# A decoder layer on one core: cross-attention's last eight pairs reordered in freed banks, and TensorE's expert slots written out

## What is computed

```
x = x + self_attention(layernorm(x))            # 16 heads, quantised weights and activations
x = x + cross_attention(layernorm(x), context)
x = x + experts(layernorm(x))                   # 8 experts, top 2, FF 688

def cross_attention(h, ctx):                    # 16 heads of width 128
    q = rmsnorm(h @ Wq) * gq                    # per head
    k = rmsnorm(ctx @ Wk) * gk;  v = ctx @ Wv
    p = softmax(q @ k.T / sqrt(128))            # 64 queries x 64 keys in each of the 32 sequences
    return (p @ v) @ Wo

def experts(x):
    top_v, top_i = top_k(x @ router_w.T, 2);  probs = softmax(top_v)
    y[e] = (silu(x @ gate[e].T) * (x @ up[e].T)) @ down[e].T
    return sum over the two chosen e of probs * y[e]
```

## Time and profile before

| | |
|---|---|
| Runs | 1113.59 us median of 3 (1110.93 to 1114.21) |
| The profiled execution | 1113.47 us; its span, first to last instruction: 1111.7 us |
| TensorE, VectorE, ScalarE, GpSimd busy in the span | 71%, 61%, 51%, 31% |
| Cross-attention's steps without projections | about 672 to 752 us of the span |
| Routing | 752 to 816 us |
| Expert slots | 816 to 1096 us |

### The profile page before, as it was taken

How to read it: one execution, slowest core, us unless ns; L and a number is a source line. 1 busy time by engine, 2 the same in 40 slices (tenths; PEclk the granted TensorE clock), 3 DMA queues, 4 the chain that set the end, 5 groups by cost and what they waited for, 6 DMA issues and landing times. The chain is left out here.

```text
span 1111.7 us, 27116 instructions
## 1 busy us (share of the span) xinstructions
PE 783.8 (71%) x10382; PEld 563.0 (51%) x10383; DVE 674.2 (61%) x1178; ACT 569.7 (51%) x863; POOL 342.0 (31%) x375
## 2 busy tenths in 40 slices
PE   0016677862336779998998997666269999999993
PEld 0015666752222235565665565556246666666662
DVE  4995788869773567778787775546833333333330
ACT  0145899983733555665666754433024444444441
POOL 0300555441420012323232323330034444444442
PEclk9997777676666999999999998995579999999997
DMA  4002666758000101101101001008265222222223
GB/s 138 0 0 77 225 243 234 253 213 317 0 0 1 36 19 27 40 3 40 41 3 40 28 15 41 2 2 313 76 255 196 36 37 37 38 38 38 38 33 95
DMA packets 40062, 90.86 MB, mean 82 GB/s; under 512 B 5264, under 2 KB 25488, under 8 KB 38128
## 3 DMA queue, kind: packets, MB, share of 16 engines
q1 hardware_dynamic: 29168, 76.22, 19.4%
q0 software_dynamic: 7488, 10.23, 5.8%
q10 hardware_dynamic: 3328, 3.28, 0.8%
HBM read 62.71 MB, written 29.10 MB: 83 GB/s over the span
## 5 line engine op out<-in xcount | busy, mean ns | idle before, releaser
L1464 DVE SCALAR_TENSOR_TENSOR hid<-psu,hid 128x688 f32<-128x688 f32 x39 | 34.1, 874 | 168.0 <-ACT hid L1328 164.2
L872 POOL TENSOR_TENSOR x_pf<-x_sc,x_rden 128x512 f32<-128x512 f32 x32 | 33.3, 1042 | 252.8 <-DVE x_rden L989 252.8
L1026 PE MATMUL xbank_q<-arena 128*128 128x512 f16 x384 | 96.5, 389 | 17.0 <-DVE q_hl L956 11.9
L1106 PE MATMUL xbank_a<-arena,x_o 128*128 128x256 f16 x768 | 95.8, 275 | 17.5 <-DVE x_o L966 17.5
L1328 ACT ACTIVATE hid<-psg 128x688 f32<-128x688 f32 x39 | 29.0, 743 | 134.8 <-PE psu L1531 134.8
L1106 PEld LDWEIGHTS xbank_a<-arena,x_o 128*128 128x128 f16 x768 | 72.7, 98 | 32.7 <-DVE x_o L966 25.0
L1531 PE MATMUL psg<-wgu,f_xT 128*128 x468 | 76.6, 314 | 16.9 <-issue 11.0
L1545 PE MATMUL fbank<-arena,hidT 128*128 (+1 forms) x702 | 87.2, 273 | 1.3 <-ACT f_y L1346 0.8
L886 ACT ACTIVATE sqq<-xbank_q 128x512 f32<-128x512 f32 x64 | 38.1, 595 | 91.8 <-PE xbank_q L1026 91.8
L1531 PE MATMUL psu<-wgu,f_xT 128*128 x468 | 75.2, 310 | 0.0
L1545 PEld LDWEIGHTS fbank<-arena,hidT 128*128 128x128 f16 (+1 forms) x702 | 63.4, 97 | 16.7 <-issue 10.2
(11 more groups left out here) (276 smaller groups left out, 1948.0 us busy)
## 6 DMA issues: line engine op xcount, KB each, us to landing
arena<-in_wgu SPq DMA_DIRECT2D x16, 688.0 KB, 5.7
gu_pair<-arena SPq DMA_DIRECT2D x16, 688.0 KB, 3.1
wgu<-gu_pair SPq DMA_DIRECT2D x8, 1376.0 KB
ao<-key_norms SPq DMA_DIRECT2D x64, 128.0 KB, 3.2
d_pair<-arena SPq DMA_DIRECT2D x16, 384.0 KB, 3.8
arena<-d_pair SPq DMA_DIRECT2D x8, 768.0 KB
arena<-in_wd SPq DMA_DIRECT2D x8, 384.0 KB, 5.5
x_sb<-in_x SPq DMA_DIRECT2D x2, 1024.0 KB, 9.4
```

What stands on the lines that cost most here:

```text
L1026: last = nc.tensor.matmul(bank_q[:, :], wq[:, a, k, f:f + D2], hT[:, b * NCH + k, at:at + GN], start=(j == 0), stop=(j == len(terms) - 1))
L1106: last = nc.tensor.matmul(acc[t // 2][:, (t % 2) * C:(t % 2 + 1) * C], o_hl[h % 2][:, a, at:at + P], wvo[:, b, e, :], start=(e == 0 and j ...
```

## The change

Cross-attention, from TAIL = 24 on. The banks of query and key projections become one tensor `qk` of two banks. The scores of pairs 0 to 24 stay in `xbank_s`, those of 25 to 31 go to `xbank_n`, which the norms have left. The weighted sums of odd heads from 47 on go to `qk`, the others to `xbank_o`; `attend(h)` then waits for the low half of head h - 2. Every engine's order in steps 24 to 31 changes, with the scores now two pairs ahead; step 23 takes pair 25's scores and softmax at its end, and the projection of head 46 moves from step 23 to step 24. In the experts TensorE's 41 slot steps are written out in Python instead of the loop, and the register with the expert's number is kept for the down product two slots later. The diff, cut to what differs in order, banks and waits (ScalarE's and GpSimd's bodies only moved into functions):

```diff
+TAIL = NPAIR - NU
...
-        bank_q, bank_k, bank_s, bank_n = (pb(f"xbank_{n}", [P, 512], F32) for n in ("q", "k", "s", "n"))
+        qk = pb("xbank_qk", [P, 2, 512], F32)
+        bank_q, bank_k = qk[:, 0], qk[:, 1]
+        bank_s, bank_n = (pb(f"xbank_{n}", [P, 512], F32) for n in ("s", "n"))
...
+        def ob_of(h):
+            return qk if h >= 2 * TAIL - 1 and h % 2 else ob
+
+        def bank_of(n):
+            return bank_s if n <= TAIL else bank_n
...
@@ gpsimd
+                    if N < TAIL:
+                        if pair(n):
+                            quotient(n)
+                        if pair(n + 1):
+                            both_norms(n + 1)
+                        if pair(n):
+                            quotient_low(n)
+                    if N == TAIL - 1:
+                        both_norms(n + 2)
+                        quotient(n + 1)
+                        quotient_low(n + 1)
+                    if N >= TAIL and pair(n + 1):
+                        if pair(n + 2):
+                            both_norms(n + 2)
+                        quotient(n + 1)
+                        quotient_low(n + 1)
@@ scalar
                     if head(2 * N - 1):
                         out_high(2 * N - 1)
+                    if N >= TAIL:
+                        if pair(N):
+                            turned_copy(N)
+                        if pair(n):
+                            quotient_high(n)
+                        if pair(N):
+                            out_high(2 * N)
+                        if pair(n + 1):
+                            exponent(n + 1)
+                        continue
...
+                    if N == TAIL - 1:
+                        exponent(n + 1)
@@ vector
                     if head(2 * N - 1):
                         out_low(2 * N - 1)
+                    if N >= TAIL:
+                        if pair(n + 1):
+                            shifted(n + 1)
+                        if pair(N):
+                            out_low(2 * N)
+                        if pair(n + 1):
+                            sums(n + 1)
+                        if N % NU == 0:
+                            residual(N // NU - 1)
+                        continue
...
+                    if N == TAIL - 1:
+                        shifted(n + 1)
+                        sums(n + 1)
@@ tensor, scores
-                    if n > 1:
+                    if 1 < n <= TAIL:
                         pe.wait_ge(pT_done, n - 1)
+                    if n == TAIL + 1:
+
+                        pe.wait_ge(rq_done, NHEAD // HB)
+                    if n > TAIL + 1:
+                        pe.wait_ge(s_read, n)
+                    bank = bank_of(n)
@@ tensor, turn_p
-                    if pair(n + 1):
+                    if n < TAIL:
 
                         pe.wait_ge(s_read, n + 2)
+                    else:
+                        pe.wait_ge(pT_done, n)
@@ tensor, attend
-                    if h:
+                    if h == 2 * TAIL - 1:
+
+                        pe.wait_ge(lq_done, NHEAD)
+                        pe.wait_ge(lk_done, NHEAD)
+                    elif h > 2 * TAIL:
+                        pe.wait_ge(ol_done, h - 1)
+                    elif h:
                         pe.wait_ge(ol_done, h)
+                    bank = ob_of(h)
@@ tensor, order
+                    if N >= TAIL:
+                        if pair(N):
+                            turn_p(N)
+                        if pair(n + 1):
+                            scores(n + 1)
+                        project_out(2 * N - 2)
+                        if pair(N):
+                            attend(2 * N)
+                        project_out(2 * N - 1)
+                        if pair(N):
+                            attend(2 * N + 1)
+                        continue
...
-                    if pair(N):
+                    if N == TAIL - 1:
+                        attend(2 * N + 1)
+                        scores(n + 1)
+                    elif pair(N):
                         project_out(2 * N)
                         attend(2 * N + 1)
@@ tensor, experts
+                expert_of = {}
+
                 def gate_up(r, n):
 
 
-                    e = pe.value_load(slot_e[0:1, bass.ds(n, 1)], min_val=0, max_val=NE - 1)
+                    e = expert_of[n] = pe.value_load(slot_e[0:1, n:n + 1], min_val=0, max_val=NE - 1)
...
                 def down(r, n):
-                    e = pe.value_load(slot_e[0:1, bass.ds(n, 1)], min_val=0, max_val=NE - 1)
+                    e = expert_of[n]
...
-                slot_rounds(pe, slot, NSLOT + 1)
+                for n in range(-1, NSLOT + 2):
+                    slot(n, n % 2)
```

More of the change, by code:

```diff
@@ L885, in query @@
                         act.wait_ge(ss_done, h - 1)
-                    nc.scalar.activation(sqq[h % 2][:, :], bank_q[:, :], ACT.Square, scale=1.0 / (H_UP * W_UP)).then_inc(sq_done, 1)
-                    nc.scalar.copy(q_hl[:, 0, slot(h), :], bank_q[:, :]).then_inc(hq_done, 1)
+                    nc.scalar.activation(sqq[h % 2][:, :], bank_q, ACT.Square, scale=1.0 / (H_UP * W_UP)).then_inc(sq_done, 1)
+                    nc.scalar.copy(q_hl[:, 0, slot(h), :], bank_q).then_inc(hq_done, 1)
                 def key(h):
@@ L913, in query_norms, with turned_copy, exponent, quotient_high @@
                                          ACT.Exp, scale=-0.5, bias=gains[:, 4:5]).then_inc(rq_done, 1)
+                def turned_copy(n):
+                    act.wait_ge(t_done, n + 1)
+                    nc.scalar.copy(pT[:, :, :, :, :].rearrange("p e l a n -> p (e l a n)"), bank_s[:, :].bitcast(F16)).then_inc(pT_done, 1)
+                def exponent(n):
+                    act.wait_ge(sub_done, n + 1)
+                    nc.scalar.activation(sc[n % 2][:, :, :], sc[n % 2][:, :, :], ACT.Exp).then_inc(exp_done, 1)
+                def quotient_high(n):
+                    act.wait_ge(pf_done, n + 1)
+                    nc.scalar.copy(p_hl[n % 2][:, 0, :], pf[:, :, :].rearrange("p a s -> p (a s)")).then_inc(ph_done, 1)
                 act.wait_ge(g_ready, 4)
@@ L926, in _ @@
                     if pair(N):
-                        act.wait_ge(t_done, N + 1)
-                        nc.scalar.copy(pT[:, :, :, :, :].rearrange("p e l a n -> p (e l a n)"), bank_s[:, :].bitcast(F16)).then_inc(pT_done, 1)
+                        turned_copy(N)
                     if pair(n):
-                        act.wait_ge(sub_done, n + 1)
-                        nc.scalar.activation(sc[n % 2][:, :, :], sc[n % 2][:, :, :], ACT.Exp).then_inc(exp_done, 1)
+                        exponent(n)
                     if pair(m):
@@ L1025, in query @@
                     for j, (k, a, b) in enumerate(terms):
-                        last = nc.tensor.matmul(bank_q[:, :], wq[:, a, k, f:f + D2], hT[:, b * NCH + k, at:at + GN], start=(j == 0), stop=(j == len(terms) - 1))
+                        last = nc.tensor.matmul(bank_q, wq[:, a, k, f:f + D2], hT[:, b * NCH + k, at:at + GN], start=(j == 0), stop=(j == len(terms) - 1))
                     last.then_inc(q_done, 1)
@@ L1033, in key @@
                     for j, (a, b) in enumerate(TERMS):
-                        last = nc.tensor.matmul(bank_k[:, :], wk[:, a, f:f + D2], cT[:, b, at:at + GN], start=(j == 0), stop=(j == 2))
+                        last = nc.tensor.matmul(bank_k, wk[:, a, f:f + D2], cT[:, b, at:at + GN], start=(j == 0), stop=(j == 2))
                     last.then_inc(k_done, 1)
@@ L1067, in scores @@
                                     at = slice(t * P + b * S, t * P + b * S + S)
-                                    last = nc.tensor.matmul(bank_s[b * S:b * S + S, e * RW + t * S:e * RW + t * S + S], q_hl[:, a, h, at], k_hl[:, c, h, at], start=(j == 0), stop=(j == 2))
+                                    last = nc.tensor.matmul(bank[b * S:b * S + S, e * RW + t * S:e * RW + t * S + S], q_hl[:, a, h, at], k_hl[:, c, h, at], start=(j == 0), stop=(j == 2))
                     last.then_inc(s_done, 1)
@@ L1092, in attend @@
                                     at = (2 * a + b) * S
-                                    last = nc.tensor.matmul(ob[:, half, at:at + S], ck[rows, l, h // H2 * 2 + a, b * CC:(b + 1) * CC],
+                                    last = nc.tensor.matmul(bank[:, half, at:at + S], ck[rows, l, h // H2 * 2 + a, b * CC:(b + 1) * CC],
                                                             pT[rows, h % 2, m, a, b * S:b * S + S], start=(j == 0), stop=(j == 2))
```

39 lines of the change are left out of this document (18 added, 21 removed).

## The result

The changed kernel takes 1073.3 us (median of 4 runs, 1070.11 to 1076.43), the one before 1112.8 in the same setting: a ratio of 0.9646, 95% interval 0.9613 to 0.9678. The forecast was 1075.5 in a range of 1068 to 1088. The profiled execution took 1073.23 us, its span is 1071.4 against 1111.7: 40.3 us less.

What follows compares the result with a forecast made beforehand. A chain of waits, no engine full, was taken to bound cross-attention's end; TensorE, with loop gaps, the expert slots. Gains of 22.5 + 15.2 = 37.7 us off 1113.5 were rounded to 1075.5 us, range 1068 to 1088.

Steps and rivals of the forecast that it cites:

- A: Whole kernel: the forecast itself, both parts gaining within their bounds, 1069 to 1081 us; chance 0.72.
- Part 2: Expert slots: written out, each takes 6.58 us instead of 7.03, a gain of 15.2 us, 3 us either way.
- Code arrival at nothing: Expert slots: about 20 more blocks of instructions to fetch, priced at no time; at most 28 us if unhidden.
- D: Expert slots: code arrival costs 0.5 us at each of 20 blocks, total 1085.5 us; chance 0.08.
- E: Expert slots: TensorE waits in full for each code block, 2.8 us each, 56 in all, total 1131.5 us; chance 0.03.
- Part 1: Cross-attention's steps from 24 on: new order and banks gain 22.5 us, bounds 18 to 24.
- VectorE has 0.1 to 0.2 us spare ... The step is TensorE's, 5.05 us: Cross-attention's end: VectorE just keeps up, so TensorE's work sets each step at 5.05 us, against 8.04 before.
- The clock: Cross-attention's end: a likely drop to 1.2 GHz after TensorE stands 3.1 us; 1 us taken off the gain.
- Rival B: Cross-attention's end: VectorE takes over, steps of 5.9 us give 5 us back, total 1080.5 us; chance 0.11.
- the ring: Old end of cross-attention: a closed chain of waits through shared output banks and one score bank, setting steps of 8.04 us.
- C: Cross-attention's end: scores stand behind GpSimd's norm product or norms, steps stay 8 us, total 1098 us; chance 0.04.
- F: Both parts: the change doesn't do what it says in either, so no change in time; chance 0.02.

Runs made afterwards that it cites:

- e4_loop4: The kernel before with four expert slots to a turn of TensorE's loop instead of two, 8 turns instead of 17: 1109.58 us, ratio 0.9978.
- e7_nosub: The changed kernel without the subtraction of the row maximum for pairs 26 to 31: 1071.57 us, ratio 0.9633.
- e5_onepair: The changed kernel with one pair of output banks for all heads, order and score banks staying changed: 1075.20 us, ratio 0.9669.
- e11_order: The changed kernel with one score bank and one pair of output banks, so the new order in the old banks: 1085.32 us, ratio 0.9768.
- e6_onebank: The changed kernel with one bank for scores and turned probabilities, order and output banks staying changed: 1081.45 us, ratio 0.9720.
- e10_bulk: The changed kernel with VectorE's sums after the key halves and ScalarE's key square before its quotient rounding, in steps with projections: 1063.88 us, ratio 0.9571.
- e1_slots: The kernel before with only the expert slots written out, cross-attention unchanged: 1096.26 us, ratio 0.9843.
- e2_cross: The changed kernel with the old expert loop and both loads of the expert's number: 1089.27 us, ratio 0.9791.
- e9_nosub_fill: The changed kernel without the subtraction for pairs 26 to 31, with head 46's projection and group 2's residual moved earlier: 1076.94 us, ratio 0.9689.
- e12_all: The changed kernel with the edits of e10_bulk and e9_nosub_fill together: 1065.04 us, ratio 0.9585.

## Why the prediction was right, and where it was not

**The total** was right, 1075.5 against 1073.3, and partly by luck: slot 0's higher clock and the 1.45 us ahead of the change add 3.7 us that no term foresaw, in the very execution that was profiled; without them it would stand at 1076.9, still in the range. The two parts together gave 37.1 us (21.8 and 15.3) where 37.7 were forecast. Three figures of the recorded working don't come out of its own terms: 1113.5 less 37.7 is 1075.8, not 1075.5; the bounds of both parts (18 to 24 and about 12 to 18 us) give 1071 to 1083 for A, not 1069 to 1081; and the last weighted sum ends at 724.2, not 723.8. None of them decides anything.

**Part 2, right in size.** 15.2 us were forecast and 15.0 + 0.3 measured (without slot 4, whose stop varies, the 33 slots behind it gain 14.7: 231.4 against 216.7); the slot takes 6.57 us (6.58 forecast), one stop stays at slot 4 (0.75 us against 0.52), the second load costs 0.03 us where it was priced at nothing. What was wrong is the reason: I read the 0.58 us "issue" at every second slot as the turn of the loop. By e4_loop4 the turn is only the smaller share, some 0.25 us, and each slot in a loop costs about 0.31 wherever it stands. The row named the place where the lag surfaced, not where it arose. The Trainium skill (Advanced Engine Details and Errata, Control Flow Timing) gives a compare-and-branch about 108 ns. The 0.25 us of a turn is some twice that, and the larger part, 0.31 us in each slot, stands where there is no branch.

**Code arrival at nothing: right** (rivals D and E). Nineteen packets more came on the instruction queue over the whole span (79 against 60; 20 forecast), and TensorE missed 0.5 of 225 us. The Trainium skill (Runtime: NRT & Kernel Launch, Instruction fetch mechanics) calls the crossing of a block mostly hidden; the trace agrees.

**Part 1, 22.5 us forecast, 21.8 measured.** The turn of pair 24 comes 9.61 us behind its scores, 9.60 forecast, after the stop of 3.19 us that was forecast as 3.1, and the one wait for the residual is there. The step that failed is "VectorE has 0.1 to 0.2 us spare ... The step is TensorE's, 5.05 us". VectorE has none to spare: its round is 5.38 us, because the subtraction, for which I took the 0.69 of the earlier trace rows, takes 1.61. In the old order GpSimd stood idle for 4.87 us up to its quotient, the subtraction among it, so the row could not show what it costs beside GpSimd; in the new order it meets GpSimd's low half or norm product in every step. This one mis-sized term cost some 2.3 us, an estimate from the rows. On the way in pair 25's subtraction takes 1.14 us and pair 26's 1.61, together 1.37 more than 0.69 each; projection 48 starts 19.77 us behind the scores of pair 24, where the forecast has 18.40 (690.95 less 672.55). The last step is 0.92 longer than it is without the subtraction. e7_nosub gives back 2.33, but it takes away the whole subtraction of pairs 26 to 31, not only what was mis-sized. Two others nearly cancel: TensorE's own step is 5.18, since scores behind a turn start after 0.55 and not 0.45 us (0.5 us over four steps), and I counted five full steps where the fifth has no scores (4.19 instead of 5.05, 0.9 us the other way).

**The clock.** The low level that I took 1 us off for is there at 682.15: that projection takes 2.74 us, 1.27 more than the others (granted clock 0.50 from 683 to 685), and the weighted sum behind it 0.82 instead of 0.52. But it cost about nothing: TensorE stands 1.92 us for the residual soon after, longer than the 1.57 lost. In e7_nosub the same projection is as slow, TensorE still waits 0.51 us for the residual behind it, and pair 26 is turned at 22.08 us, where the forecast without the clock has 22.15 (694.7 less 672.55). The residual's wait hid the whole of it.

**Rival B** happened, in a mild form: VectorE takes over, but at 5.38 us and not at 5.9, since the low half of head 2N fills the wait for the exponent. It gave back 2.3 us and not 5. It named the right engine for the wrong reason.

**"The change cuts both" links of the ring** was right as a description, but the new banks aren't what most of the gain came from. e5_onepair shows that the second output banks are worth 0.8 us beside the rest, and e11_order that the order alone brings over half of part 1. C and F had no part: the steps are nowhere near 8 us, and both parts do what they say.

## What to carry to other kernels

When a ring of short steps is broken up, first ask what each engine's order alone gives, since a bank added to a good order may be worth little. A duration read in a stretch where GpSimd is idle is no price for a stretch where it isn't: for a VectorE operation with both operands in SBUF take the row where the two overlap. A gap called "issue" at a loop's turn shows where the sequencer's lag surfaced, and one kernel with another number of slots per turn tells whether the turn or the slots made it.

## What the runs showed of the hardware that was not expected

**VectorE and GpSimd wait for each other.** In the step shown above the subtraction begins at 703.16 beside GpSimd's low half (703.06 to 704.22) and ends at 704.77, 0.55 us after it; the norm product, marked from 704.18, ends at 705.69, 0.92 after the subtraction. Both were lengthened, each by about the time in which the other was at work. The subtraction reads two operands from SBUF; VectorE's other two-input operations in the step, with one operand in PSUM, stay at 0.68 beside the same GpSimd work. The subtraction took up to 1.61 us in the kernel after, 1.18 in most steps of e5_onepair, 0.81 in most of e6_onebank, where the two engines meet for a shorter time, and 0.69 where they don't meet; without it the norm product is 1.06 again (e7_nosub). No run took GpSimd's operation away instead, but in two steps of the kernel after the norm product is under way before the subtraction begins. One of them:

```profile
692.40 1.06 POOL L872 TENSOR_TENSOR ao<-ao,rec_q 128x512 f32<-128x512 f32 x1
692.57 1.44 DVE L1026 TENSOR_TENSOR x_sc<-x_sc,x_mx 128x512 f32<-128x512 f32 x1
```

There the product keeps its 1.06 us, and only the subtraction grows. In the traces of the kernel after, e5_onepair, e6_onebank and e10_bulk it is the same at every meeting: a GpSimd operation that is under way when the subtraction begins keeps its time, and a lengthened subtraction ends 0.54 to 0.55 us after the GpSimd operation that was ahead of it, however long it had been waiting. Where the two meet for only 0.08 us (e11_order) it keeps 0.69.

The Trainium skill (SBUF — State Buffer, Who interferes with whom) states that a VectorE instruction with two SBUF inputs contends with a GpSimd one that reads SBUF, and calls the shared port pair an exclusive lock. For VectorE's two-port modes it adds that whoever issues first has the pair for the whole instruction while the other blocks. The trace agrees with the first, with 1.61 and 1.51 us where they meet and 0.69 and 1.06 where they don't; what it shows of who goes first, for this operation, is the pair of rows above.

**Slot 0's clock.** The matmuls of slot 0's gate take 3.62 us in the kernel before and 1.92 after, the lower (1.2 GHz) and the higher (2.4 GHz) clock level; the routing code in front is the same, as is the standing of TensorE before it (7.07 and 7.06 us, then 3.3 us of work). Of the fourteen profiled executions, one for each kernel, seven have slot 0 at 7.3 to 7.9 us and seven at 5.6. Writing the slots out doesn't decide it (7.82 in e1_slots, 5.60 in e2_cross). All seven short ones have the new end; the long ones are the three kernels with the old end and four with the new (e7_nosub, e9_nosub_fill, e11_order, e12_all). With one profile for each kernel the runs can't tell whether this is chance or goes with what came before. It is 2.2 us that a comparison of two single profiles should set aside, and what decides it stays open.

**Slot 4's stop.** The pitch of slot 4 is 7.3 to 9.2 us in all kernels, under the transfers of the expert weights. Beside slot 0's clock it is the largest thing that varies in the expert stage, and no experiment was made on it.
